# The causal mask of the diagonal score chunks: written into PSUM by ScalarE instead of by an identity product on TensorE

## The reference

```python
x = _layernorm(x + _L0_attn_ref(x, ...))   # causal, 16 heads of 8
x = _layernorm(x + _L0_ffn_ref(x, ...))    # 8 experts, top 2, relu
x = _layernorm(x + _L1_attn_ref(x, ...))   # causal, 16 heads of 8, q and k through rank 64
x = _layernorm(x + _L1_ffn_ref(x, ...))    # attention (not causal, 16 heads of 4), then 8 experts, top 2, gelu
```

```python
attn = scale * jnp.einsum('bhqd,bhkd->bhqk', q, k)
attn = jnp.where(causal[None, None], attn, -jnp.inf)
attn = jax.nn.softmax(attn, axis=-1)
```

## Time and profile before

| what | value |
|---|---|
| median of 3 runs | 1213.9 us (1211.96 to 1216.73) |
| the profiled execution | 1214.44 us, span 1212.7 us |
| mean granted TensorE clock in it | 0.985 |
| busy: TensorE, VectorE, ScalarE, GpSimd | 1108.5, 870.5, 777.6, 270.3 us |
| instructions | 24956 |

### The profile page before, as it was taken

The page is one execution under the profiler, slowest core; times in us unless marked ns, Lnnn a source line. Parts: engine busy times, 40 slices in busy tenths (PEclk is TensorE's granted clock), DMA queues, the critical chain, the costliest instruction groups (busy, mean ns, idle before and its releaser), DMA issues. The chain is left out here.

```text
span 1212.7 us, 24956 instructions
## 1 busy us (share of the span) xinstructions
PE 1108.5 (91%) x8799; PEld 605.9 (50%) x8872; DVE 870.5 (72%) x2077; ACT 777.6 (64%) x1563; POOL 270.3 (22%) x819
## 2 busy tenths in 40 slices
PE   8899998999999988999988998888888898899996
PEld 6466665656766655666655642221112221137774
DVE  4888887773434377888766899899999889904433
ACT  4376766667444436777666667888888778874443
POOL 4244332332002013533233421111110011000001
PEclk9899999999999999999999999999999989999999
DMA  7245431110001701243211321102111000000000
GB/s 192 57 111 135 113 93 32 40 32 2 1 1 23 165 11 41 74 104 95 71 48 58 62 39 33 29 12 35 37 33 29 20 12 16 7 1 1 10 9 18
DMA packets 39550, 57.67 MB, mean 48 GB/s; under 512 B 9393, under 2 KB 14977, under 8 KB 39041
## 3 DMA queue, kind: packets, MB, share of 16 engines
q1 hardware_dynamic: 39424, 56.06, 18.7%
HBM read 30.81 MB, written 24.64 MB: 46 GB/s over the span
## 5 line engine op out<-in xcount | busy, mean ns | idle before, releaser
L864 ACT ACTIVATE probs<-bank 128x512 f32<-128x512 f32 x1088 | 574.6, 601 | 235.2 <-PE bank L1261 234.2
L980 DVE TENSOR_REDUCE tile_max<-bank 128x1 f32<-128x512 f32 (+3 forms) x1152 | 612.3, 593 | 38.0 <-PE bank L1246 33.3
L1246 PE MATMUL bank<-qk 125*128 125x128 bf16 (+2 forms) x1664 | 389.0, 312 | 59.1 <-DVE tile_max L980 46.7
L1261 PE MATMUL bank<-qk 128*128 128x128 bf16 (+4 forms) x1607 | 362.8, 306 | 5.7 <-ACT probs L864 5.3
L1290 PE MATMUL bank<-probs,v_head 128*32 128x512 f32 (+3 forms) x3328 | 304.3, 454 | 0.1
L1246 PEld LDWEIGHTS bank<-qk 125*128 125x128 bf16 (+1 forms) x1664 | 132.2, 97 | 316.9 <-DVE tile_max L980 244.2
L1147 DVE SCALAR_TENSOR_TENSOR acc<-bank,gate,acc 128x128 f32<-128x128 f32 x256 | 72.0, 344 | 156.7 <-PE bank L1417 156.7
L1290 PEld LDWEIGHTS bank<-probs,v_head 128*32 128x32 f32 x3328 | 139.7, 109 | 52.8 <-issue 29.8
L1261 PEld LDWEIGHTS bank<-qk 128*128 128x128 bf16 (+1 forms) x1664 | 133.2, 97 | 56.8 <-ACT probs L864 21.0
L884 ACT ACTIVATE probs<-bank,sb_b 128x512 f32<-128x512 f32 x128 | 81.0, 684 | 117.9 <-PE bank L1406 117.9
L974 DVE TENSOR_REDUCE tile_max<-bank 128x4 f32<-128x512 f32 x128 | 87.4, 688 | 87.0 <-PE bank L1246 86.7
(11 more groups left out here) (133 smaller groups left out, 659.8 us busy)
## 6 DMA issues: line engine op xcount, KB each, us to landing
qk<-qk_parts SPq DMA_DIRECT2D x160, 144.0 KB
qk_parts<-q_parts SPq DMA_DIRECT2D x48, 192.0 KB, 2.4
qk_parts<-k_parts SPq DMA_DIRECT2D x48, 192.0 KB, 3.0
qk_parts<-q_parts SPq DMA_DIRECT2D x24, 96.0 KB, 2.3
qk_parts<-k_parts SPq DMA_DIRECT2D x24, 96.0 KB, 2.9
sb_w<-in_w SPq DMA_DIRECT2D x8, 256.0 KB, 3.8
sb_w<-in_w SPq DMA_DIRECT2D x2, 1024.0 KB, 5.6
qk<-neg_rows SPq DMA_DIRECT2D x96, 6.0 KB
```

The source lines that it names most:

```text
L864: nc.scalar.activation(probs[:, hd.probs_place(c), :], S2[i % len(S2)][:], ACT.Exp, scale=hd.a.scale).then_inc(sem("probs"), 1)
L980: ins = nc.vector.tensor_reduce(tile_max[:, hd.slot, t, which:which + 1], s1[:, at:at + P * count], AX.X, ALU.max)
L1246: ins = mm(s1[:, at:at + P * count], qk[hd.query_rows, hd.place, 0, P * t:P * (t + 1)], qk[hd.query_rows, hd.place, 1, P * k0:P * (k0 + co ...
L1261: ins = mm(s2[:, at:at + P * count], qk[hd.key_rows, hd.place, 1, P * j:P * (j + 1)], qk[hd.key_rows, hd.place, 0, P * q0:P * (q0 + count) ...
```

## The change

For 58 of the 64 causal heads (all but the first three of each run) the two products of identity and mask are left out. Instead ScalarE copies `mask16` into the bank, in float32, behind the probabilities of chunk 6 (for diagonal chunk 0) and of chunk 8 (for diagonal chunk 1) of the head three earlier, when VectorE has read the bank. TensorE waits for the count `seeded` and issues the four products with `start` off, so that they add to what stands in the bank. With that, the second product of a chunk of two pieces has `start` off too.

```diff
--- before.py
+++ after.py
@@ -85,6 +85,10 @@
     def query_diagonal(self, c):
         return self.causal and c < 2
 
+    def seed_behind(self, c):
+
+        return (6, 8)[c]
+
 
 ATTENTIONS = [Attention(0, 8, 8, True), Attention(1, 8, 8, True), Attention(2, 4, 4, False)]
 
@@ -151,6 +155,18 @@
         return CHUNKS[run.stop]
     there, here = HEADS[g + AHEAD].a.chunks, HEADS[g].a.chunks
     return CHUNKS[g + AHEAD] + -(-(c + 1) * there // here)
+
+
+
+SEED_AHEAD = AHEAD + 1
+
+
+def seeded(g):
+
+    return HEADS[g].a.causal and g - SEED_AHEAD >= RUNS[g >= NH].start
+
+
+SEEDS = [2 * sum(seeded(g) for g in range(h)) for h in range(3 * NH + 1)]
 
 
 def query_chunk(i):
@@ -840,6 +856,13 @@
                 ge(act, f"max_in{g % RING}", 16 * (g // RING))
                 nc.scalar.activation(neg_rows[:, g % RING, :], neg_ps, ACT.Copy).then_inc(sem("neg_rows"), 1)
 
+            def seed(g, c):
+
+                i = CHUNKS[g] + c
+                act.wait_ge(sem("max_taken"), i + 1 - len(S1))
+                nc.scalar.activation(S1[i % len(S1)][:], mask16[:].rearrange("p t k -> p (t k)"), ACT.Copy
+                                     ).then_inc(sem("seeded"), 1)
+
             def take_sums(i):
                 act.wait_ge(sem("pv"), BATCHES[GROUPS[i][-1].g + 1])
                 ge(act, "out", i - 1)
@@ -863,6 +886,10 @@
                         ge(act, "pv", pv_before(g, c))
                         nc.scalar.activation(probs[:, hd.probs_place(c), :], S2[i % len(S2)][:], ACT.Exp,
                                              scale=hd.a.scale).then_inc(sem("probs"), 1)
+                        if g + SEED_AHEAD < run.stop and seeded(g + SEED_AHEAD):
+                            for diagonal in range(2):
+                                if c == hd.a.seed_behind(diagonal):
+                                    seed(g + SEED_AHEAD, diagonal)
                         before = at_place_before(run, g, k)
                         if c == batch[hd.read_after] and before is not None:
                             between(before)
@@ -1236,8 +1263,13 @@
                 if c == 0:
                     pe.wait_ge(sem(f"qk_in{hd.slot}"), qk_loaded(hd))
                 ge(pe, "max_taken", i + 1 - len(S1))
+
                 first = True
-                if a.query_diagonal(c):
+                if a.query_diagonal(c) and seeded(g):
+
+                    pe.wait_ge(sem("seeded"), SEEDS[g] + c + 1)
+                    first = False
+                elif a.query_diagonal(c):
                     mm(s1[:], ident16[:], mask16[:].rearrange("p t k -> p (t k)"), start=True, stop=False,
                        skip_group_check=True)
                     first = False
```

## The result

The changed kernel takes 1251.63 us (median of 5 runs, 1250.65 to 1252.28) against 1213.9; the ratio is 1.0308, with a 95% interval of 1.0296 to 1.032. I had forecast 1240 with a range of 1222 to 1254, so the direction and the range held, and the loss came out at 38 us instead of 26. Its profiled execution has a span of 1248.4 us, 35.7 more than before.

The account below looks back on a forecast made before the run. TensorE's in-order work was taken to bound the causal heads; 29 x (0.59 + 0.32) = +26.4 us on the profiled 1214.4 gave 1240.8, stated as 1240 us (+2.2%), range 1222 to 1254.

Parts of the forecast that it names:

- The mechanism: First diagonal chunk: TensorE waits for the seed behind chunk 6's probabilities, starting 0.81 us (even) or 0.54 us (odd heads) later.
- The signs: Profile after: 12 mask products, TensorE waiting for a seed once a head, 45 to 50 us, none at second diagonal chunk.
- what I had worked out: Whole kernel: the summed waits and saved masks hold as counted, giving 1232 to 1246 us; chance 50%.
- the rival on GpSimd: Even heads: late by_quarter makes TensorE wait for maxima, 12 us; seeds may lengthen other stages' chains; 1246 to 1262, chance 20%.
- The seed of 0.60 us: ScalarE's copy of the 128x512 mask into a PSUM bank, taken as 0.60 us from a same-size copy to SBUF.
- the 0.22 us of a hidden product: Second diagonal chunk: the seed is ready in time, so the 0.22 us of TensorE's mask product are won.
- the mean growth of a steady head: Causal heads: first-chunk wait less the saved mask, +0.59 us in an even head and +0.32 in an odd one.
- the 0.06 us from the seed's end to the product: First diagonal chunk: TensorE sees the end of ScalarE's seed 0.06 us later, as with a VectorE wait before.
- `by_quarter`'s delay: Even heads: ScalarE's copy starts 1.31 us later, GpSimd's maxima steps end at 114.13, 0.07 us left; counted zero.
- the mean of the sum: All 58 seeded heads: even +0.59 and odd +0.32 us, counted also for heads with other stages' steps.
- one rival: Wait partly absorbed: some 20 heads waiting for other stages hide loss, 9 us; shorter seed 10 us; 1220 to 1232, chance 18%.
- Seeds in time: Both diagonal chunks: seeds are ready before TensorE needs them, both masks won, 25.5 us less, 1188 us; chance 7%.

Follow-up runs that it names:

- e1: The changed kernel with only diagonal chunk 1's mask written by ScalarE, chunk 0's back on TensorE; 1209.8 us, ratio 0.9948 to the kernel before.
- e2: The changed kernel with only diagonal chunk 0's mask written by ScalarE, chunk 1's back on TensorE; 1256.3 us, ratio 1.0331 to the kernel before.
- e3: The changed kernel with TensorE making all masks and ScalarE's 116 copies going to unused SBUF, awaited by nobody; 1223.0 us, ratio 1.0062 to before.
- e4: The changed kernel with the seed of chunk 0 behind chunk 5's probabilities instead of chunk 6's; 1235.5 us, ratio 1.0167 to the kernel before.
- e10: The changed kernel with TensorE's wait for the seed named ahead of its two other waits; 1246.9 us, ratio 1.0274 to the kernel before.
- e12: The kernel before the change with only the six bias steps moved; 1214.2 us, ratio 1.0007 to the kernel before.

## Why the prediction was right, and what it missed

*The mechanism* held: TensorE waits at chunk 0 for a seed that stands behind chunk 6's probabilities, and everything behind it in TensorE's order moves. e1 and e2 part the two seeds, e3 shows that ScalarE's load alone costs 7 to 8 us and not 38, e4 that an earlier seed gives loss back, in steady heads in the forecast amount. The signs came, with one exception: a wait at chunk 0 in each of the 58 heads, 52.0 us in all (forecast 45 to 50), and 12 mask products left; but in three heads there is also a wait at the second diagonal chunk, where I had forecast none.

*The number* was helped by a wide range. 1251.6 us lies outside the 1232 to 1246 that I gave 50% for what I had worked out, and inside the 1246 to 1262 of the rival on GpSimd, whose wait for `neg_parts` stayed at 3.6 us. The 9 to 11 us above the forecast have other causes:

*The terms.* The seed of 0.60 us measured 0.605; the 0.22 us of a hidden product 0.21 to 0.22 in e1; the mean growth of a steady head, forecast at +0.59 and +0.32 us, measured +0.68 and +0.41.

*The term that was too small in each head* is the 0.06 us from the seed's end to the product. I took it from a wait that stands on the weight load itself; the seed's wait stands on an instruction before it, and it measured 0.14 to 0.15. With e10's order it is 0.06, and the steady heads grow by 0.60 and 0.34, as the sum had it. In all 58 x 0.08 = 4.6 us.

*The step that was missing*: I followed `by_quarter`'s delay to GpSimd's last step on the maxima, found 0.07 us left and stopped. That rival did not come in the changed kernel (TensorE's wait for `neg_parts` 3.6 us in three times), though e3 shows it lurking. But I didn't ask what else stands in GpSimd's order behind it. The bias step does, and it met VectorE's `a_tok`: 5 heads x 0.5 = 2.5 us.

*The heads with other stages' steps*: +0.61 where the mean of the sum was 0.45, and 0.53 with the correction of 0.08; 22 x 0.08 = 1.8 us more. Two rivals meet here. Some of the loss is hidden, as one rival had it: heads 19, 25, 52 and 57 grow by less than 0.1 us. And chains are lengthened, as another had it: behind head 22 TensorE waits 1.74 us for the seed of chunk 0, at the second diagonal chunks 1.6 us in three heads, and for `neg_parts` in heads 27 and 53 0.7 and 0.6 us longer than before. Which step of which chain is late in each of the 22 heads was not settled. 4.6 + 2.5 + 1.8 = 8.9 us of the 9.3 between 26.4 and the span's 35.7.

*The rivals.* Seeds in time: right for chunk 1 in all but a few heads, and wrong for chunk 0; with only the one that is in time the kernel is faster, as that rival priced it per product. I had judged the two seeds together.

## What to carry to other kernels

Work moved from a full engine to one with 30% free costs by its place in that engine's order: ask when the last instruction ahead of it ends, not how busy the engine is, and price each moved piece alone (here one of two gains 0.22 us a head, and the other loses 0.9 or 0.6). Where an instruction waits for several semaphores, see to it that the one that comes last stands on the instruction itself (here by naming it first). When a step becomes late, follow the whole queue of each engine behind it to steps that share something with another engine, not only to the one that is awaited. And before two traces are compared by the length of a stage, look at the granted clock in it.

## What the runs showed of the hardware

- A product whose weight load carries the late wait starts 0.06 us after the other engine's end; with the late wait on the instruction ahead, 0.14 to 0.15 us (e10 and the changed kernel: the order of the waits alone differs; 58 heads each). The profile then sometimes names the wrong engine: half of the time was put down to VectorE, whose maxima of chunk 6 had been done for 1.3 us in head 8 when the load began.
- VectorE's product of two SBUF inputs of 128x128 took 0.29 us alone. Beside GpSimd's addition of 1.28 us it took 0.46 to 1.29 us and ended 0.15 us after it in all 30 cases; GpSimd's step was not longer.
- ScalarE's copy of 128x512 from `mask16` took 0.605 us to PSUM (the changed kernel) and 0.642 to SBUF (e3). Back to back its activations started 0.47 to 0.52 us apart in head 8 of the changed kernel, seeds included.
- At the lower granted clock (0.5) products of one bank came 0.43 us apart instead of 0.21 or 0.22; one such stretch of 3.4 us made e12's head 23 1.64 us longer.
